# Order of TensorE's stream at the start, at each group's split and around the tail windows, sums of one group by halves, tail sums kept in their PSUM bank

## The reference

```python
attn = softmax((x Wq)(x Wk)^T * V**-0.5)          # within each batch of 32 rows
attn_out = (attn (x Wv)) Wp + bp
cms_out = gelu(attn_out cW1 + cb1) cW2 + cb2 + one_hot(code)
modifier = gelu([attn_out, cms_out] mW1 + mb1) mW2 + mb2    # inner width 1024
x1 = clip(x + cms_out + modifier, 0, 1)
# three adapters, each with the weights of the batch's role:
y = x + gelu(x W_down + b_down) W_up + b_up       # 256 -> 128 -> 256
x = layernorm(y) * gamma + beta
```

## Time and profile before

| | us |
|---|---|
| median of three runs | 366.13 |
| runs | 367.71, 366.13, 365.42 |
| the profiled execution | 363.89 |
| its span, first to last instruction | 362.1 |
| TensorE busy in it | 348.7 (96%) |
| VectorE busy | 197.0 (54%) |
| ScalarE busy | 166.4 (46%) |
| GpSimd busy | 62.0 (17%) |

### The profile page before, as it was taken

The page is one execution under the profiler, slowest core; times in us unless marked ns, Lnnn a source line. Parts: engine busy times, 40 slices in busy tenths (PEclk is TensorE's granted clock), DMA queues, the critical chain, the costliest instruction groups (busy, mean ns, idle before and its releaser), DMA issues.

```text
span 362.1 us, 6606 instructions
## 1 busy us (share of the span) xinstructions
PE 348.7 (96%) x2232; PEld 282.9 (78%) x2232; DVE 197.0 (54%) x477; ACT 166.4 (46%) x333; POOL 62.0 (17%) x94
## 2 busy tenths in 40 slices
PE   7889999999999999999999999999999999999994
PEld 6677688677876867888786777877899999989962
DVE  5057365420332746763535766554579777553584
ACT  3465685432652555452326454443455554533421
POOL 2700230000040101001311111003322025100231
PEclk9999999999999999999999999999999999999999
DMA  6663799175020223220076797602856543298001
GB/s 209 202 229 119 200 106 162 11 213 130 2 58 0 60 80 97 69 79 0 29 242 159 208 264 241 172 29 80 207 151 191 160 107 98 66 295 310 16 2 44
DMA packets 30646, 46.14 MB, mean 127 GB/s; under 512 B 4779, under 2 KB 15348, under 8 KB 30612
## 3 DMA queue, kind: packets, MB, share of 16 engines
q1 hardware_dynamic: 28852, 41.72, 42.6%
q0 software_dynamic: 1392, 3.80, 3.6%
q10 hardware_dynamic: 368, 0.20, 0.2%
HBM read 43.60 MB, written 4.48 MB: 133 GB/s over the span
## 4 chain that ended last, share of the span: by engine, by line
PE 85%; ACT 5%; DVE 4%; issue 3%; POOL 2%; DMA 1%; POOLq 0%; DVEq 0%; ACTq 0%
PE bank L312 11%; PE bank L314 10%; PE bank L313 10%; PE bank L1353 8%; PE bank L1358 8%; PE bank L1354 7%; PE bank L1277 4%; PE bank L1397 4%; PE bank L1376 3%; PE bank L1228 2%; PE bank L1267 2%; PE bank L1248 2%; ACT h_full L760 2%; PE bank L1428 2%; ACT h_hi L764 1%
## 5 line engine op out<-in xcount | busy, mean ns | idle before, releaser
L760 ACT ACTIVATE h_full<-bank,bias 128x512 f32<-128x512 f32 (+1 forms) x80 | 48.2, 602 | 114.4 <-PE bank L314 109.6
L985 DVE TENSOR_TENSOR h_lo<-h_full,h_hi 128x512 fp32r<-128x512 f32 (+1 forms) x80 | 46.7, 584 | 65.1 <-ACT h_hi L764 63.6
L683 POOL TENSOR_TENSOR rstd<-moments,minus_half 128x1 f32<-128x1 f32 x39 | 24.3, 624 | 174.2 <-DVE moments L1039 174.2
L764 ACT ACTIVATE h_hi<-h_full 128x512 fp32r<-128x512 f32 (+1 forms) x80 | 43.7, 546 | 2.6
L1031 DVE TENSOR_TENSOR window_y<-bank,window_x 128x256 f32<-128x256 f32 x39 | 16.5, 423 | 42.6 <-PE bank L1376 34.8
L1353 PE MATMUL bank<-h_hi,m_hi 128*128 128x512 f32 (+1 forms) x80 | 31.1, 397 | 0.4 <-ACT h_hi L764 0.3
L1353 PE MATMUL bank<-h_hi,c_hi 128*128 128x512 f32 (+1 forms) x80 | 30.8, 395 | 0.1
L312 PE MATMUL bank<-at_hi,m_hi 128*128 128x512 f32 (+1 forms) x80 | 29.5, 369 | 0.0
L312 PE MATMUL bank<-at_hi,c_hi 128*128 128x512 f32 (+1 forms) x80 | 29.4, 367 | 0.0
L314 PE MATMUL bank<-at_lo,c_hi 128*128 128x512 f32 (+1 forms) x80 | 27.8, 348 | 0.0
L314 PE MATMUL bank<-at_lo,m_hi 128*128 128x512 f32 (+1 forms) x80 | 27.8, 347 | 0.0
(11 more groups left out here) (216 smaller groups left out, 717.9 us busy)
## 6 DMA issues: line engine op xcount, KB each, us to landing
adapter_w<-packed_w SPq DMA_DIRECT2D x48, 256.5 KB, 3.5
adapter_rows<-packed_rows SPq DMA_DIRECT2D x36, 256.0 KB, 3.7
mixed_w<-packed_w SPq DMA_DIRECT2D x12, 256.5 KB, 4.6
stage<-in_L_cond_mW SPq DMA_DIRECT2D x6, 512.0 KB, 4.7
stage<-in_L_cond_cW SPq DMA_DIRECT2D x4, 512.0 KB, 6.5
last_w<-packed_w SPq DMA_DIRECT2D x2, 769.5 KB, 5.8
up_bias<-in_L_cond_b_up SPq DMA_DIRECT2D x12, 128.0 KB, 5.5
adapter_rows<-packed_rows SPq DMA_DIRECT2D x24, 64.0 KB, 3.2
```

What stands on the lines that cost most here:

```text
L683: pool.tensor_tensor(slot.rstd[:, :], slot.moments[:, 1:2], minus_half[:, :], ALU.pow)\
L760: act.activation(h_full[:, n % 2, rows], bank[n % 2][:, rows], ACT.Gelu, bias=bias[:, b:b + 1])\
L764: act.activation(h_hi[:, n % 2, rows], h_full[:, n % 2, rows], ACT.Copy).then_inc(h_hi_ready, 1)
L985: dve.tensor_tensor(h_lo[:, n % 2, rows], h_full[:, n % 2, rows], h_hi[:, n % 2, rows].bitcast(F32), ALU.subtract).then_inc(h_lo_ready, 1)
```

## The change

Six edits, in the words of the code:

1. In `core`, D(7) and C stand ahead of Ha(8) and Ha(9), so that D(6) and D(7) are neighbours.
2. At the start, the turns of the first half (X 0) stand ahead of the second folding, and those of the second half (X 1) ahead of Y 0, on TensorE and on ScalarE. A product of 64 columns that nothing reads (L1177) is gone.
3. F and E of group 2 work in two parts of 256 rows: add and clip the first, then add and clip the second. `x1_needed` and the counts that wait for sums follow (`sum_parts`, `summed`).
4. The up bias of a tail is put into its sum bank by an identity product (`last_bias`), the turn of `xT` becomes a product that adds to it (`last_first_sum`), and up adds to that. VectorE's add (`last_sum`) and the residual product of layer 0 go.
5. Window 13's bias, sum and down stand behind Hb(9), ahead of D(8).
6. Behind the last D, the bias products of windows 14 and 15 stand on both sides of window 13's second up.

```diff
-        core += [("D", HB - 2), ("Ha", HB), ("D", HB - 1), ("C", 0), ("Ha", HB + 1), ("Hb", HB), ("Hb", HB + 1)]
+        core += [("D", HB - 2), ("D", HB - 1), ("C", 0), ("Ha", HB), ("Ha", HB + 1), ("Hb", HB), ("Hb", HB + 1)]
...
+        def sum_parts(g):
+
+            return 2 if g + 1 in CARRIED and GROUPS[g][1] == GR else 1
...
+                if step in ("F", "E"):
+                    share = size // sum_parts(g)
+                    for part_n in range(sum_parts(g)):
+                        rows = slice(part_n * share, (part_n + 1) * share)
+                        cols = slice(first + part_n * share, first + (part_n + 1) * share)
...
-            def last_sum(tail):
-                dve.wait_ge(tail.loaded, 16 * tail.loads)
-                dve.wait_ge(tail.turned, 1)
-                if tail.left:
-                    dve.wait_ge(*tail.left)
-                dve.tensor_tensor(tail.x[:, :], tail.sum_bank[:, 0:V], tail.up_bias[:, :], ALU.add).then_inc(tail.x_ready, 1)
-
...
-            keep_busy(1, P // 2)
...
+            def last_bias(n):
+                tail = last[n]
+                pe.wait_ge(tail.loaded, 16 * tail.loads)
+                pe.matmul(tail.sum_bank[:, 0:V], ident[:, :], tail.up_bias[:, :], start=True, stop=False)
+
             def last_first_sum(n):
                 tail, w = last[n], LAST[n]
                 for vb in range(VB):
-                    ins = pe.transpose(tail.sum_bank[:, vb * P:(vb + 1) * P], xT[:, vb, columns(w)], ident[:, :])
-                ins.then_inc(tail.turned, 1)
+                    pe.matmul(tail.sum_bank[:, vb * P:(vb + 1) * P], xT[:, vb, columns(w)], ident[:, :],
+                              start=False, stop=False)
...
+            half_part("X", 0)
             pe.wait_ge(wT_copied, 3)
...
-            half_part("X", 0)
+            half_part("X", 1)
             half_part("Y", 0)
-            half_part("X", 1)
             half_part("Y", 1)
...
-                if g == NM - 1 and step == ("D", HB):
+                if g == NM - 1 and step == ("Hb", HB + 1):
 
                     pe.wait_ge(cms_copied, VB * NM)
-                    pe.wait_ge(last[0].loaded, 16 * last[0].loads)
+                    last_bias(0)
                     pe.wait_ge(x1_ready, x1_needed(LAST[0]))
+                    last_first_sum(0)
                     last_down(0, 0)
-                    last_first_sum(0)
                 if g == NM - 1 and step == ("D", HB + 2):
-                    last_residual(0, 0)
                     last_up(0, 0)
```

More of the change, by code:

```diff
@@ L356, in build, with summed @@
                 steps.append((g, step))
+        def sum_parts(g):
+            return 2 if g + 1 in CARRIED and GROUPS[g][1] == GR else 1
+        def summed(g):
+            return VB * sum(sum_parts(n) for n in range(g))
         ATTENTION = {0: {("H", 10): ("X", 2), ("H", 11): ("Y", 2), ("H", 13): ("S", 2), ("H", 14): ("P", 2),
@@ L444, in x1_needed @@
         def x1_needed(w):
-            return PRIMED + VB * next(n + 1 for n, (first, rows) in enumerate(GROUPS) if (w + 1) * P <= first + rows)
+            n, (first, rows) = next((n, group) for n, group in enumerate(GROUPS) if (w + 1) * P <= sum(group))
+            part = ((w + 1) * P - first - 1) * sum_parts(n) // rows
+            return PRIMED + summed(n) + VB * (part + 1)
         def result_banks(g, n):
@@ L1007, in part @@
                     dve.wait_ge(base_ready, VB * (g + 1))
[L1008 to L1015, removed]
+                if step in ("F", "E"):
[3 more added lines that the diff above has]
+                        cols = slice(first + part_n * share, first + (part_n + 1) * share)
+                        if step == "F":
+                            for vb in range(VB):
+                                dve.scalar_tensor_tensor(cms[:, vb, rows], result_banks(g, HB)[vb][:, rows],
+                                                         bias[:, MB2 + vb:MB2 + vb + 1], xT[:, vb, cols], ALU.add, ALU.add)\
+                                    .then_inc(mod_summed, 1)
+                        if step == "E" or sum_parts(g) > 1:
+                            for vb in range(VB):
+                                dve.wait_ge(mod_summed, summed(g) + VB * part_n + vb + 1)
+                                dve.tensor_scalar(xT[:, vb, cols], cms[:, vb, rows], 0.0, 1.0, ALU.max, ALU.min)\
+                                    .then_inc(x1_ready, 1)
             def before(wave, spot):
@@ L1078, in last_norm @@
                 dve.wait_ge(tail.rstd_ready, tail.base + layer + 1)
+                if layer == 0 and tail.left:
+                    dve.wait_ge(*tail.left)
                 dve.scalar_tensor_tensor(tail.x[:, :], tail.y[:, :], tail.rstd[:, :], tail.rows[layer][:, 1, :],
@@ L1099, in _ @@
                     part("E", 0, g - 1)
-                if g + 1 in CARRIED and step == ("F", 0):
+                if g + 1 in CARRIED and step == ("F", 0) and sum_parts(g) == 1:
                     part("E", 0, g)
@@ L1121, in _ @@
                     dve.wait_ge(eps_ready, 2 * SLOTS)
-                if g == NM - 1 and step == ("H", HB + 2):
-                    last_sum(last[0])
                 if g == NM - 1 and step == ("H", HB + 4):
@@ L1173, in _, with keep_busy @@
             pe.wait_ge(ident_ready, 1)
-            def keep_busy(n, columns=P):
+            def keep_busy(n):
                 for _ in range(n):
-                    pe.matmul(bank[6][:, 0:columns], ident[:, :], ident[:, 0:columns], start=True, stop=True)
+                    pe.matmul(bank[6][:, 0:P], ident[:, :], ident[:, :], start=True, stop=True)
             keep_busy(2)
@@ L1523, in _ @@
             for n in (two_, three):
-                pe.wait_ge(last[n].loaded, 16 * last[n].loads)
                 last_down(n, 0)
                 last_first_sum(n)
-            for n in (two_, three):
-                last_residual(n, 0)
-                last_up(n, 0)
+            last_up(two_, 0)
+            last_up(three, 0)
             last_turn(one, 2)
```

30 lines of the change are left out of this document (15 added, 15 removed).

## The result

The changed kernel is slower: 368.47 us median of 20 runs against 365.11 of 20 runs of the kernel before, ratio 1.0073 (95% interval 1.0047 to 1.0099), about 2.7 us. The ratio is worked out for itself, without the few runs in which the chip was in a slower state, and is not the quotient of the two medians, which lie 3.4 us apart. On the chip of the last experiments the same comparison gave 1.0043 (1.0010 to 1.0076). The forecast was 365.9 with a range up to 368.1. It took three runs of the kernel before as its level, 366.13; the median of 20 is 1.0 us lower. So the level hides 1.0 us of the miss: forecast was a change of -0.23 us, measured was one of about +2.7.

The account below looks back on a forecast made before the run. TensorE, busy 348.7 of 362.1 us, was taken as the bound. Terms -0.2 - 0.57 - 0.05 - 0.39 + 0.93 + 0.05 = -0.23 us, from the 366.13 median to 365.9; range 364.0 to 368.1.

Parts of the forecast that it names:

- The start, -0.2: Start: reordering X and the second folding about even (-0.12), removing the small product -0.1; together -0.2 us.
- Against it: Argument against a clock fall at the start: TensorE does nothing from 358 to 362 us, yet granted clock stays 1.00.
- The first rival: Start: idling from 11.86 to 14.5 us lets the clock fall or rise late, +4.1 us; chance 0.1.
- three stages of eight passes: Start: at the low clock each of three such stages would cost 1.36 us more, together +4.1 us.
- The small product's -0.1: Start: removing the product at 7.25 us lets the gathers start sooner, -0.1 us, between 0 and -0.5.
- The split: D(7) directly after D(6) in five groups: Hb(8) of group 0 stops waiting, -0.57 us; group 4 -0.05.
- Groups 3 and 4: D(7) moved earlier: 0 in group 3, no cms wait there; -0.05 us in group 4, where VectorE is late.
- Halves: Group 2 sums: window 8's down starts 0.77 us sooner, a later h_lo gives part back; -0.39 us net.
- Window 13: Group 4: bias product ahead of D(8) waits 1.4 us for its load; H(10) +1.36, net +0.93 us.
- The end: Tails 14 and 15: adds and residual products go, bias and sum products come; +0.05 us, between -0.7 and +0.4.

Follow-up runs that it names:

- window 13 back: Changed kernel with window 13's bias, sum and down behind D(8) again: 364.79 us, ratio 1.0015 to the kernel before.
- its wait filled: Changed kernel with 8 products that nothing reads in the wait for window 13's up bias: 365.79 us, ratio 1.0025 to the kernel before.
- the split alone: Kernel before with only the new order of D(7) and C ahead of Ha(8) and Ha(9): 362.49 us, one run.
- the filler: The 8 products that nothing reads, put into the changed kernel's wait for window 13's up bias: 365.79 us, ratio 1.0025.
- the new start alone: Kernel before with only the new start order, without the small product: 366.77 us, ratio 1.0092.
- 12 products: Changed kernel with 12 products that nothing reads in front of X 0: 364.50 us, ratio 1.0021 to the kernel before.
- all three places held: Changed kernel with products that nothing reads at the start and in window 13's wait, and one-column products in three portions: 363.81 us, ratio 0.9980.
- the halves alone: Kernel before with only group 2's sums added and clipped in two parts: 363.41 us, one run.

## Why the prediction was wrong, point by point

**The start, -0.2: the step that failed.** The order was priced rightly: with the clock held, X 0 to scores takes 7.2 to 7.3 us in both orders. What failed is "Against it: at the end TensorE does nothing from 358 to 362 and the granted clock stays 1.00". One stretch was read as a rule. It ended too soon: in the kernel before TensorE's last product ends at 357.35 and the clock falls at 362.3, just behind the last instruction (0.77 is the mean of four us with the fall in them):

```profile
362.00:366.00 4.00, 0.00 (x0) 0.00 (x0) 0.00 (x0) 0.00 (x0) 0.00 (x0) 0.77 0.00 0
```

With the old start restored, TensorE ends at 355.7 and the clock is down from 357.7, while in the changed kernel 4.8 us of nothing still read 1.00. In all 18 profiles the clock comes down between 1.7 and 5.2 us behind the last product.

```profile
355.80:357.60 1.80, 0.00 (x0) 0.00 (x0) 1.52 (x5) 0.00 (x0) 0.55 (x1) 1.00 0.28 80
357.70:360.50 2.80, 0.00 (x0) 0.00 (x0) 0.03 (x1) 0.00 (x0) 0.00 (x0) 0.50 0.18 48
```

```profile
361.40:366.20 4.80, 0.00 (x0) 0.00 (x0) 1.68 (x5) 0.00 (x0) 0.55 (x1) 1.00 0.23 65
```

What the clock does behind an idle stretch differs between executions; one reading of 1.00 excludes nothing. With the new start order and nothing put into the wait, it fell for 4.09 us of idle time in the changed kernel and for 3.87 and 2.70 in two versions of it (window 13 back, its wait filled), and stayed for 0.95 in the second profile of the changed kernel: how long TensorE idles depends on when the gather lands. The first rival's mechanism came true, both its forms (fall, late rise), in a part of the executions and for one or two of its three stages of eight passes: 1.8 us in the profile, 1.3 to 1.7 by the runs, where it had 4.1 and a chance of 0.1. The Trainium skill, "TensorE: Matmul & The Clock Gate", Part 1, has an idle array return to 1.2 GHz; the changed kernel's 0.50 behind 4.09 us of idle time agrees. The small product's -0.1 is not shown: over the profiles the first gather is issued from 8.23 to 8.63 us without it (mean 8.36) and from 8.45 to 8.67 with it (8.54), but X 0, which waits for the landing, starts between 12.7 and 14.6 either way.

**The split.** -0.57 in group 0 measured -0.61: right. Groups 3 and 4, taken as 0 and -0.05, gave -0.28 and -0.29; in the split alone window 13's loads, which the prediction let move along with TensorE's stream, took 0.81 back.

**Halves**, -0.39: -0.58. The first part was in time as said; h_lo gave back 0.20, not 0.38.

**Window 13**, +0.93: right in mechanism, mis-sized. One part is a misreading: the chain's row at 325.42, taken as the start of H(10) before, is what the chain keeps of that pass behind the one ahead of it; in the timeline H(10) starts at 325.17. The same sum from there gives +1.61 and a net of +1.18. The wait was 1.92 us, not 1.4, since the landing did not keep its place: 2.07 us behind the start of Hb(9)'s last pass instead of 1.61, and the split had shortened the stream ahead of it. In the trace the net is +1.42; by the runs undoing the place is worth 1.9 to 2.1 us. Part of that can be clock, as two of five profiles show; the filler did not prove it for the median.

**The end**, +0.05: +0.16.

**Not in the sum at all:** the clock lost behind the one-column block, 1.7 us in the changed kernel's profile. On which edit it is to be booked, if on any, is open. With the block whole, all six profiles of the changed kernel and of the versions that keep its start order have the fall. None of the six with the old start order has it, nor has the one with the new start alone. But it is not there in every execution of the new order: three of the 12 runs with 12 products have a mean clock of 0.996 or more, too high for such a stretch. And the kernel before also loses clock somewhere in some of its runs (their mean clock goes down to 0.983). No experiment moved the start and the block apart to tell an effect from chance.

By the trace of the changed kernel the terms add up: start +1.87, the fall behind the block +1.7, the rest of the way to window 8's down (the split, small waits) -0.1, the halves with their give-back -0.6, groups 3 and 4 -0.5, window 13 +1.4, end +0.2: 4.0, as seen. Of the 2.7 us of the ratio, the runs show a start of 1.3 to 1.7 and a window 13 of about 2, against about 1 gained by the rest; each of these is uncertain by about 1 us. That the version with all three places held comes out at 0.9980, near the predicted -0.23 us, is partly luck: window 13 cost 0.5 us more than its term, and groups 3 and 4 and the halves gave 0.6 more than theirs.

## What to carry to other kernels

An idle stretch on the engine that bounds a kernel has two prices: the time, and the clock of the work behind it. Work that stands in a wait is worth more than its own length: it keeps the clock, so moving it out to fill another gap can lose where a plain count of idle time comes out even. Ahead of such a move, ask what TensorE does while it waits now, and if nothing, put in products that nothing reads, short enough to end before the wait does. In this kernel 12 of them at the start were worth about 1.3 us, 17 made it no better, and in the short waits of the old start and at window 13 the median did not fall. And a wait moved ahead on an in-order queue should come with the transfer it waits for moved ahead too.

## What was not expected of the hardware

- TensorE's clock can fall with no idle time at all: in a row of 72 one-column passes it went from 2.4 to 1.2 GHz and stayed there for over 13 us, through 4.7 us of full passes at the end. A block of 24 (2.6 us) does it in some executions and not in others; in three portions it was in no profile.
- The same kernel, the same place: behind 0.95 us of idle time at the start the clock stayed, behind 4.09 it fell. With the old start order, 1.31 and 0.69 us of idle time went with a fall in one version, 1.55 and 0.69 in another (the halves alone) with none. In the three versions with both the start filled and the block in portions, executions lie within 0.9 to 2.1 us of one another; the changed kernel's 20 lie within 5.4.
- Seven loads of 128 to 256 KB issued in a row: over the profiles the last landed 5.1 to 6.1 us after its issue; the up bias, put at the head of the row, landed after 3.5.
